# A GNN kernel: when VectorE copies the next window's gather indices, and the last layer's node rows

## The reference

```
m      = relu(h[src] + edge_attr @ eencW + eencb) + 1e-7
logits = m * t
e      = exp(logits - segment_max(logits, dst)[dst])
agg    = segment_sum(m * e / segment_sum(e, dst)[dst], dst)
h'     = relu(layernorm((agg + h) @ W1 + b1)) @ W2 + b2
x      = x + h'          # layer 0: x = h';  then h = relu(layernorm(x)) for the next layer
```

## Time and profile before

| | us |
|---|---|
| runs | 11806.76, 11829.9, 11827.7; median 11827.7 |
| profiled execution: its own time | 11828.1 |
| profiled execution: span of the instructions | 11826.3 |

### The profile page before, as it was taken

One profiled execution on the slowest core, in us unless ns is written; L12 is line 12 of the kernel. 1 busy time (PEld: TensorE's weight loads), 2 busy tenths in 40 slices (PEclk: granted clock), 3 DMA queues, 4 the chain that ended last, 5 costly groups with the idle time before them and its releaser, 6 DMA issues. The chain is left out here.

```text
span 11826.3 us, 107787 instructions
## 1 busy us (share of the span) xinstructions
PE 5802.2 (49%) x31762; PEld 4077.1 (34%) x31762; DVE 6551.7 (55%) x8055; ACT 3327.1 (28%) x4948; POOL 6522.0 (55%) x6157
## 2 busy tenths in 40 slices
PE   2333333343444444444444444444444447888887
PEld 2222222232333333333333333333333334444443
DVE  5666666664444444544444445444444457998897
ACT  1333333342333333333333333333223232111110
POOL 5455455535444444454544444544444446888887
PEclk6666666666666666666666666666666668999998
DMA  5344344333333333333333333333333334555555
GB/s 155 125 137 138 123 140 132 130 109 103 118 117 117 117 117 117 102 97 116 119 118 118 117 118 106 95 117 118 117 117 117 117 112 94 99 97 99 96 94 86
DMA packets 840467, 1354.58 MB, mean 115 GB/s; under 512 B 499934, under 2 KB 556476, under 8 KB 838730
## 3 DMA queue, kind: packets, MB, share of 16 engines
q1 hardware_dynamic: 523832, 1135.94, 27.5%
q0 software_dynamic: 312640, 214.30, 12.9%
q10 hardware_dynamic: 3916, 3.40, 0.1%
HBM read 806.66 MB, written 546.46 MB: 114 GB/s over the span
## 5 line engine op out<-in xcount | busy, mean ns | idle before, releaser
L826 POOL DMA_INDIRECT xg<-h_tab,idx x4656 | 4461.7, 958 | 4370.0 <-DVE idx L1159 2909.3
L917 PE MATMUL turn<-hb,hot 125*128 125x192 bf16 x12480 | 1872.5, 295 | 3018.0 <-issue 2977.7
L917 PEld LDWEIGHTS turn<-hb,hot 125*128 125x128 fp8e4 x12480 | 1310.6, 114 | 3571.7 <-issue 3536.0
L1159 DVE COPY idx<-idx_full 128x24 int32 x208 | 36.6, 176 | 3526.7 <-ACT zl L1035 3526.7
L933 PE MATMUL turn<-ident,sums 128*128 128x128 f32 x5184 | 1073.7, 375 | 1533.8 <-ACT st_all L1050 1140.4
L1524 POOL DMA_INDIRECT acc<-vm,tgt x1026 | 1602.9, 1562 | 341.2 <-issue 288.1
L933 PEld LDWEIGHTS turn<-ident,sums 128*128 128x128 f32 x5184 | 878.0, 222 | 1676.3 <-ACT st_all L1050 1243.6
L1066 ACT ACTIVATE hx<-turn 128x384 bf16<-128x384 f32 x156 | 76.4, 490 | 3600.9 <-PE turn L917 3553.1
L1050 ACT ACTIVATE st_all<-turn 128x512 f32<-128x512 f32 (+1 forms) x1344 | 752.3, 577 | 698.7 <-PE turn L933 321.0
L1166 DVE TENSOR_TENSOR_SCAN rx<-rp,carry,zl 128x1536 f32<-128x1536 bf16 (+1 forms) x224 | 739.9, 3303 | 360.1 <-ACT zl L1035 343.1
L1597 PE MATMUL zl<-spreadz,lo_hot 128*128 128x512 f32 x1620 | 765.5, 609 | 95.2 <-DVE spreadz L1773 95.2
(11 more groups left out here) (277 smaller groups left out, 7413.2 us busy)
## 6 DMA issues: line engine op xcount, KB each, us to landing
sums<-st_all SPq DMA_DIRECT2D x208, 1536.0 KB
hot<-hot_tab SPq DMA_DIRECT2D x312, 625.0 KB
ea<-feat SPq DMA_DIRECT2D x158, 768.0 KB
srcB<-src_flat SPq DMA_DIRECT2D x108, 768.0 KB
rp<-run_pen SPq DMA_DIRECT2D x210, 384.2 KB
xg<-h_tab,idx POOLq DMA_INDIRECT x4656
hot_tab<-hot SPq DMA_DIRECT2D x104, 625.0 KB
run_head<-zeros SPq DMA_DIRECT2D x216, 192.0 KB
```

The source lines that it names most:

```text
L826: g_.indirect_dma_start(xg[b][:, k, h, :], None, h_tab[:, :], bass.IndirectOffsetOnAxis(ap=idx[b][:, h, k:k + 1] if small is None else idx ...
L917: ins = pe.matmul(picked[:, :, n % 2, :], hot[n][0:PN, t_, :], hb[0:PN, t_, :, :], start=t_ == 0, stop=t_ == NT - 1, skip_group_check=True)
```

## The change

Three edits:

1. In DVE's `window`, for every full window, `next_lists(w + 2, b)` moves ahead of the wait for `l_ok`. In its place as a guard stand three waits, for the gathers of window w (`xg_in[b][gr]`). The two old places of the copy (layers 1 to 3, and layer 0) go.
2. SP no longer stores the node rows behind the last layer.
3. SP's wait at the end for the stores counts the stores of three layers, and a wait for the last layer's `h_ok` is added.

```diff
-                        for k in range(NCH):
+                        for k in range(NCH if l + 1 < L else 0):
                             sp.wait_ge(h_ok, NCH * l + k + 1)
                             store_nodes(k)
...
-                    sp.wait_ge(tab_out, 16 * NCH * L + 16)
+                    sp.wait_ge(tab_out, 16 * NCH * (L - 1) + 16)
+                    sp.wait_ge(h_ok, NCH * L)
...
                         link = Chain(v, dve_step, g * STEPS)
+                        if width == W:
+                            for gr in range(NG):
+                                v.wait_ge(xg_in[b][gr], xg_count(l, i, GT, gr))
+                            next_lists(w + 2, b)
                         v.wait_ge(l_ok, g + 1 + L0)
-                        if width == W and l:
-                            next_lists(w + 2, b)
                         link(v.tensor_tensor_scan(rx[:, 0:width], rp[b][:, 0:width], zl[:, 0:width], carry[:, 0:1], ALU.min, ALU.max))
...
-                        if width == W and not l:
-                            next_lists(w + 2, b)
                         v.tensor_copy(wmax[:, w:w + 1] if isinstance(w, int) else wmax[:, bass.ds(w, 1)], segmax[:, 0:1])
```

## The result

The changed kernel takes 11060.27 us (median of 4, 11056.71 to 11067.33) against 11825.72 for the kernel before (4 runs): ratio 0.9356, 95% interval 0.934 to 0.9373, 765 us less. The forecast was 11,338 and its range began at 11,110: the direction and the place were right, but the gain was forecast at 488 us where 765 came.

A forecast was written before the change was run, and what follows sets the result against it. No engine was above 55% busy; a cycle of gathers, PE's resume, rest of `select`, `forward` and next gather was the bound. 11828.1 - 338 (layers 1 to 3) - 150 (layer 0) - 2 (last node rows) = 11338 us; range 11,110 to 11,760.

The forecast's parts named there:

- The cycle: Layers 1 to 3: gather to PE's resume 31.3 us, rest of `select` 3.0, `forward` to next gather 8.1; sum 42.4.
- The 8.1 us: Layers 1 to 3: time from `forward` by way of ACT, scan and copy to the next gather, forecast to become 1.8.
- What comes back: Layers 1 to 3: earlier burst leaves 45 matmuls of `select` at PE's resume, 6.9 us; period 40.0, 338 us less in all.
- `back` starved: Rival, layers 1 to 3: the burst catches `back`, all 80 matmuls of `select` follow; 12,445 us, or 12,130 in half; chance 0.08.
- the loop's jump: Rival: PE's jump ahead of `forward` in every second window loses its instruction store; mean period 46.5 us, 12,460 us; chance 0.03.
- the copy is still late: Rival: DVE's chain is drawn out by ACT's exponentials behind a slowed `back`; half the gain left, 11,580 us; chance 0.11.
- Layer 0: Copy moves ahead of the scan; DVE's waits put the period at 41.6 us, 3.0 less: 150 us, ends 0 and 310.
- The last node rows: End of the last layer: eleven issues of SP go; 1.5 us less, between 0 and 3.
- The range: Whole kernel: 11,110 to 11,760 us, with the half gain inside and the conserved case nearly reached.
- a store of instructions: PE: about 58 matmuls with their weight loads, not refilled while gathers are issued nor for 3.9 us after.

The follow-up runs named there:

- e6: Changed kernel with four of 22 gathers left out of every full window of layers 1 to 3: 10274.76 us, 0.8685 of the kernel before.
- e7: Changed kernel with one hot column instead of two (23 gathers, 40 matmuls of `select` a window): 10561.4 us, 0.8929 of the kernel before.
- e15: Kernel before with the copy moved in layers 1 to 3 alone: 11136.46 us against 11794.01, ratio 0.9444.
- e1: Kernel before with the copy moved in layers 1 to 3 alone, where the kernel before took 8777.24 us: 8776.35 us, ratio 0.9998.
- e2: Kernel before with the copy moved in layer 0 alone, where the kernel before took 8777.24 us: 8791.94 us, ratio 1.0018.
- e8: Kernel before with the copy moved in layers 1 to 3 alone, run again: 8777.25 us, where the kernel before took 8777.33.
- e5: The changed kernel, unaltered, run again: 11072.6 us against 11836.07 for the kernel before, ratio 0.9358.

## Why the prediction was half right

**The cycle** (first gather, resume, rest of `select`, `forward`, next gather): right. The gather to resume stayed 31.4 us for 22 gathers and moved with their number (e6, e7). That the copy leaves the path and `z_ps` ends the wait: right, against the row of L827. The 8.1 us became 1.41, where 1.8 was taken from eight transposes at the lower clock; the clock is up by then, and they take 1.04. That is 0.4 us of the error in a period.

**What comes back**: the failed step. It said "36 took 5.52 us, 19 took 3.01, 0.154 each: 6.9 us". Measured are 42 left in 4.85 us, 2.0 us less. The count was nearly right (45 forecast: 25 done before the stretch and 10 in it; 32 and 6 came; the 19.7 us given for ten single ones is 19.3 by the earlier trace rows, and nothing hangs on it) and makes 0.5 of the 2.0. The price was wrong and makes 1.6: it held all 45 to the lower clock, where the changed kernel's clock rises behind the 18th and the other 24 take 0.083 us each. Both rows that I had were of matmuls that ran at 1.2 GHz to their end or nearly. The 19 of the earlier trace rows were over before the clock rose, and the 36 of the earlier trace rows met a late rise, 5 us after the resume. That the same matmul stood 0.08 us apart ahead of the slowed stretch was in the prediction, and not used.

But the rows of the kernel before wouldn't have given the whole of it either: with their median rise of 4.3 us the 42 would have taken some 5.6 us (an estimate: 27 at 0.16, 15 at 0.083). That the rise comes earlier in the changed kernel is luck as far as this forecast goes, and its cause is open.

The Trainium skill (TensorE: Matmul & The Clock Gate, Part 1) says that the array comes out of idleness at 1.2 GHz, and that the point of the rise varies by 0.5 us either way. The traces agree with the first (granted clock 0.50 at the resume); the point varies by more here, from 2.7 to 6.0 us after the resume in nine of ten windows of the changed kernel.

Together 2.0 + 0.4 = 2.4 us a period, 353 us in 147 periods. The spans of layers 1 to 3 give 650 us of gain for the 338 forecast, 312 more and not 353, because the mean period before was 41.9 us from scan to scan and not 42.3: 4.3 us of gain a period where 2.3 was forecast.

**`back` starved, the loop's jump**: neither came. All 24 matmuls of `back` and some 32 of `select` run ahead of the first single one. From the first gather on these are 55 to 62 in all 147 windows (median 58, as before), while the first single one comes anywhere from 12.8 to 25.7 us after that gather (a median 8.6 before): what runs out is a count, not a time. Windows behind the loop's jump and the others have the same median period within 0.15 us. The scan chain of DVE is as long as before, so in layers 1 to 3 "the copy is still late" didn't come either: in no full window of the loop is it the last wait (the copy stands a median 12 us ahead of the gather).

**Layer 0**: forecast -150, measured -129 in the traces and some -100 by e15. The reason given, DVE, was half of it. Timeline of the changed kernel, a window of layer 0, PE, then POOL, then DVE:

```profile
1304.97 1.97 PE L876 MATMUL turn<-ident,ea 128*64 128x128 f32 x16 [18.27 <-ACT at L1023]
1306.88 3.97 PE L883 MATMUL zl<-at,attrW 128*128 128x512 f32 x6
1310.68 1.51 PE L902 MATMUL zl<-ident,xg 128*128 128x128 f32 x12
```

```profile
1299.23 0.96 POOL L827 DMA_INDIRECT xg<-h_tab,idx  x1 [0.30 <-issue]
1313.15 0.95 POOL L827 DMA_INDIRECT xg<-h_tab,idx  x1 [12.96 <-PE zl L902]
```

```profile
1312.00 0.18 DVE L1160 COPY idx<-idx_full 128x24 int32 x1 [0.17 <-DVE hot L1204]
1317.41 3.42 DVE L1169 TENSOR_TENSOR_SCAN rx<-rp,carry,zl 128x1536 f32<-128x1536 bf16 x1 [5.23 <-ACT zl L1036]
```

It is the same cycle as in the other layers: from the last gather's end 4.8 us until ACT lets the last third of L876 go, its 2 us, the encoding 4. `forward` begins 10.1 us behind the gathers on the mean of 49 windows, where I had taken 6.6 from one of them for the lower end. Behind it the view names PE as the one that ended POOL's wait, but the copy at 1312.00 did: 1.15 us later comes the gather, exactly as in the earlier trace rows (4541.57 to 4542.72), and 1.41 us behind `forward` it would have been 1312.1. The copy stands behind the tables there, and decides in about half of the 49 windows, a little over 1 us late each, some 30 us in all. So the copy is late in layer 0, though not by the way that the rival named: DVE stands 5.5 us ahead of the tables (L1204, at 1300.94), where its code waits for DMAs that the slowed SP issues, and not for the exponentials.

**The last node rows**: 1.6 us for the 1.5 forecast. It repeats: from ACT's last chunk of node rows to POOL's first instruction of the last part it is 2.4 us in every kernel that was profiled with the stores (before, e1, e2, e8, e15) and 0.9 in those without. The table's last row, +14, wasn't forecast. It lies between the layers. The gathers of the first three windows of a layer now run as one burst of 66 (44 before), and from the burst's begin to the layer's first scan it is 67, 75 and 64 us (61, 64 and 66 before). I take the one for the cause of the other, but no run separates them, and layer 3 doesn't show it.

**The range** assumed the price of 0.154 at both ends of the count, so its lower end was too near. Nor did the forecast's chances have a case in which what is left costs less than that.

## What to carry to other kernels

When work moves across a stretch in which TensorE is idle, price it by the rows at either clock and ask on which side of the rise it falls; a mean over a short burst may not be stretched. Measure on more than one occasion before you tune to a cycle: the stall that made this edit worth 6.4% was absent in three of six groups of runs, and there the same edit costs 0.15%. The cost is the copy's 0.3 us on DVE's path in all 50 windows of layer 0, where the prediction counted 18. And where the bound differs by level, the best split between gathers and matmuls differs too (one hot column: 0.893 and 1.012).

## What the runs showed of the hardware

The same program took 11,701 to 11,836 us or 8,775 to 8,777, and one chip showed both. At the longer times PE gets through about 58 matmuls after a burst's first gather and then runs single ones, 0.7 to 4.5 us apart, until 3.3 to 4.0 us after the last gather's end (medians of the kernels). SP is slowed with it: three of its DMAs stand 0.6 and 1.2 us apart in a period of e2 (3741.60, 3742.24, 3743.44) and 7.1 and 7.2 us in one of the changed kernel (3744.80, 3751.87, 3759.08). At the other level 80 matmuls run through beside the gathers. The gathers themselves are alike, 1.257 us apart, and the part of the program behind the layers takes 2031 us in the kernel before and 2023 in e1, so nearly all of the difference lies in the layers.

I called what runs out a store of instructions that isn't refilled. The count of 58 fits that, but no refill is in the traces: at both levels the profile has the same 36 packets of 16 KB of its queue for instructions, and in the traces of before, the changed kernel, e1 and e5 none of its packets falls between the 4th and the 49th window of a layer. So what holds the instructions back stays open, and so does what sets the level. I hadn't asked in the prediction whether the slowed stretches belong to the kernel or to the machine's condition, and every price in it depends on that.
